# Two attention layers on 128 graphs: value products of two units in one run, output projections spread over the steps

## The reference

```python
# layer 0
nx = _ln(x, ln1_g, ln1_b)
q, k, v = nx @ wq + bq, nx @ wk + bk, nx @ wv + bv        # 8 heads of 32
bias = where(adj > 0, 0.1 * adj * adj, -inf)
attn = softmax(q k^T / sqrt(32) + bias)
x1 = x + ((attn v) @ wo + bo)
x2 = x1 + gelu(_ln(x1, ln2_g, ln2_b) @ w1 + b1) @ w2 + b2   # 256 -> 1024 -> 256
# layer 1, on x2
q, k, v = x2 @ Wq + bq, x2 @ Wk + bk, x2 @ Wv + bv
attn = softmax(where(adj == 0, -inf, q k^T / sqrt(32)))
y = (attn v) @ Wo + bo + x2
out = (y - mean) * rsqrt(var + eps) * gamma + beta
```

## Time and profile before

| what | value |
|---|---|
| runs | 2198.92, 2195.23, 2197.36 us; median 2197.36 |
| profiled execution | 2197.36 us, span 2195.3 us |
| mean granted clock of TensorE | 0.988 of full |
| data moved | 75.74 MB, mean 35 GB/s |
| costliest group | ScalarE's exponentials, 2048 of 393 ns |
| second | GpSimd's products with the inverse, 512 of 1064 ns |

### The profile page before, as it was taken

One profiled execution on the slowest core, in us unless ns is written; L12 is line 12 of the kernel. 1 busy time (PEld: TensorE's weight loads), 2 busy tenths in 40 slices (PEclk: granted clock), 3 DMA queues, 4 the chain that ended last, 5 costly groups with the idle time before them and its releaser, 6 DMA issues.

```text
span 2195.3 us, 58908 instructions
## 1 busy us (share of the span) xinstructions
PE 2150.0 (98%) x20300; PEld 1859.5 (85%) x20300; DVE 1802.1 (82%) x8414; ACT 1683.8 (77%) x5646; POOL 1155.7 (53%) x1266
## 2 busy tenths in 40 slices
PE   8899999999999999999999999999999999999986
PEld 6688888888888888888888888888888888888875
DVE  6688888888888888888888888888888888888774
ACT  5578787778777778877778877788877787877773
POOL 4345655445655455655455555455555455555454
PEclk9999999999999999999999999999999999999997
DMA  4010111011111001111101110101111001110000
GB/s 128 25 35 28 40 33 40 23 31 35 40 33 36 27 28 38 37 36 31 32 28 38 34 39 31 33 26 40 33 40 31 30 28 40 33 40 29 22 14 17
DMA packets 94309, 75.74 MB, mean 35 GB/s; under 512 B 8129, under 2 KB 93761, under 8 KB 94017
## 3 DMA queue, kind: packets, MB, share of 16 engines
q1 hardware_dynamic: 94016, 71.99, 10.7%
HBM read 55.20 MB, written 16.78 MB: 33 GB/s over the span
## 4 chain that ended last, share of the span: by engine, by line
PE 95%; DVE 2%; issue 1%; ACT 1%; POOL 0%; DMA 0%; SPq 0%; POOLq 0%; DVEq 0%
PE p_bank L1124 67%; PE p_heads L1221 10%; PE p_heads L1208 8%; PE p_bank L1240 7%; PE p_bank L1143 4%; ACT scores L650 1%; DVE normed L883 0%; DVE x_two L768 0%; DVE probs_t L920 0%; ACT normed L661 0%; DMA scores<-in_L_gnn_wk 0%; DVE scores L861 0%; DVE adj_c L814 0%; SPq L440 0%; POOL w_up L374 0%
## 5 line engine op out<-in xcount | busy, mean ns | idle before, releaser
L650 ACT ACTIVATE scores<-scores,negmax 128x128 f32<-128x128 f32 x2048 | 793.7, 393 | 25.4 <-DVE negmax L861 25.0
L585 POOL TENSOR_TENSOR scores<-scores,inverse 128x512 f32<-128x512 f32 x512 | 541.9, 1064 | 339.6 <-DVE inverse L872 339.6
L650 ACT ACTIVATION_READ_ACCUMULATOR scores<-scores,negmax 128x1 f32 x2048 | 392.2, 192 | 0.0
L1124 PEld LDWEIGHTS p_bank<-w_down,hidden 128*128 128x128 f32 x3072 | 374.7, 190 | 8.6 <-issue 6.0
L1124 PE MATMUL p_bank<-w_down,hidden 128*128 128x256 f32 x3072 | 381.8, 284 | 0.0
L1124 PE MATMUL p_bank<-normed,w_up 128*128 128x512 f32 x1536 | 370.3, 397 | 1.9 <-DVE normed L883 1.9
L1124 PEld LDWEIGHTS p_bank<-normed,w_up 128*128 128x128 f32 x1536 | 285.0, 189 | 67.6 <-issue 8.4
L1221 PE MATMUL p_heads<-ident,scores 128*128 128x128 f32 x2048 | 313.1, 276 | 8.3 <-DVE negmax L861 3.5
L861 DVE CUSTOM_DVE_ANT_0 scores<-p_heads,adj_a 128x128 f32<-128x128 f32 x1024 | 235.2, 286 | 43.7 <-issue 43.7
L1221 PEld LDWEIGHTS p_heads<-ident,scores 128*128 128x128 f32 x2048 | 241.2, 141 | 35.0 <-DVE negmax L861 11.1
L673 ACT ACTIVATE p_bank<-p_bank,ready_cols 128x512 f32<-128x512 f32 x256 | 169.5, 662 | 131.4 <-PE p_bank L1124 125.9
(11 more groups left out here) (117 smaller groups left out, 3704.5 us busy)
## 6 DMA issues: line engine op xcount, KB each, us to landing
res_a<-in_x SPq DMA_DIRECT2D x32, 512.0 KB, 3.8
out<-res_c SPq DMA_DIRECT2D x128, 128.0 KB, 1.7
x_in<-in_x SPq DMA_DIRECT2D x31, 512.0 KB, 3.8
adj_a<-in_adj SPq DMA_DIRECT2D x32, 256.0 KB, 2.9
adj_c<-in_adj SPq DMA_DIRECT2D x32, 256.0 KB, 2.9
piece_room<-in_L_gnn_w SPq DMA_DIRECT2D x2, 512.0 KB, 8.1
x_two<-in_x SPq DMA_DIRECT2D x1, 512.0 KB, 5.5
res_c<-in_L_gnn_w SPq DMA_DIRECT2D x1, 512.0 KB, 6.3
```

The lines of the kernel that those rows point to most:

```text
L585: nc.gpsimd.tensor_tensor(rows_g, rows_g, inverse[:, step % 2, heads].unsqueeze(2).broadcast_to([P, HC, P]), ALU.mult).then_inc(probs_made, 1)
L650: last = nc.scalar.activation(scores[:, k % 2, h], scores[:, k % 2, h], ACT.Exp, scale=-1.0, bias=negmax[:, k % 2, h:h + 1], accum_out=tot ...
L1124: last = nc.tensor.matmul(dst, stationary(i), moving(j), start=(n == 0), stop=(n == total_n - 1))
```

## The change

V of two units stands in one run, in the odd steps: in step r, V of units r-3 and r-2, and W of unit r-3; W of unit r-2 follows in step r+1. So V and W of the first unit of a pair come one step later than before, V of the second in the same step as before, and its W one step later. Step 1 has both projections of its pair and step 2 has none, so that stage A is complete when the MLP begins. In step 2 the second projection of values (`V A 1`) moves from behind T1 to ahead of T0. Probabilities and heads get a second buffer each (`probs_t`, `heads_t`), and the copies of heads take the 512 columns of both units at once. The normalization for stage M of units 2 and 3 is in step 2 (unit 2 was at the end of step 1). `late` is made from the new places of W as before, so normalization, gain, shift and store of a unit of C come a step later too. SyncE's code is not touched. The core of the diff:

```diff
-    by_step = {}
+    by_step = {k: [] for k in steps}
     for r, k in enumerate(steps):
-        by_step[k] = ([("V", r - 2), ("W", r - 2)] if r >= 2 or pending else []) + (
-            [("T", r - 1)] if r >= 1 or pending else [])
+        by_step[k] += [("T", r - 1)] if r >= 1 or pending else []
+        by_step[k] += [("W", -3)] if r == 0 and pending else []
+        if r % 2 and (r >= 3 or pending):
+            by_step[k] += [("V", (r - 3, r - 2)), ("W", r - 3)]
+            if r == 1:
+                by_step[k] += [("W", r - 2)]
+            elif r < len(steps) - 1:
+                by_step[steps[r + 1]] += [("W", r - 2)]
...
-        early = {1: ("Q", "A", 0), 2: ("V", "A", 0), 4: ("DOWN", 1), 6: ("Q", "C", 0), 7: ("V", "C", 0)}
+        early = {1: [("Q", "A", 0)], 2: [("V", "A", 0), ("V", "A", 1)], 4: [("DOWN", 1)], 6: [("Q", "C", 0)],
+                 7: [("V", "C", 0)]}
...
-        probs_t = sb("probs_t", [P, H, P])
-        heads_t = sb("heads_t", [P, 2, KC, P], F32R)
+        probs_t = sb("probs_t", [P, 2, H, P])
+        heads_t = sb("heads_t", [P, 2, 2, KC, P], F32R)
...
-                nc.scalar.activation(heads_t[:, HI].rearrange("p c n -> p (c n)"), p_bank[bank][:, 0:KC * P],
+                nc.scalar.activation(heads_part(HI, units), p_bank[bank][:, 0:len(units) * KC * P],
...
-                    if k == 2:
-                        for r in s.late.get(k, []):
-                            apply_norm(t, r, GB - 1)
+                    if k == 2 and s.m and s.pending:
+                        apply_norm(t, -1, 2)
+                        apply_norm(t, -1, 3)
...
+            def value_products(t, units):
...
+                for i, r in enumerate(units):
+                    _, _, b = t.unit(r)
+                    for h in range(H):
+
+                        j, c = h % HC, h // HC
+                        last = nc.tensor.matmul(dst[HD * j:HD * (j + 1), (i * KC + c) * P:(i * KC + c + 1) * P],
+                                                values[room(t, stage)][:, b, h * HD:(h + 1) * HD],
+                                                probs_t[:, parity(r), slot_of(c, j), :], start=True, stop=True)
+                last.then_inc(filled[bank], 1)
```

More of the change, by code:

```diff
@@ L88, in __init__ @@
         self.lag, self.tail = lags(self.steps, pending, drain)
-        self.late, waiting = {}, [-3] if pending else []
+        self.pending = pending
+        self.late, waiting = {}, []
         for k in self.steps:
@@ L136, in __init__, with use_units @@
         assert not self.looped or len(self.use) % BANKS == 0
+    def use_units(self, r):
+        return [use[1] for use in self.use if use[0] == "O" and use[1][0] == r]
     def number(self, ops):
@@ L409, in turned_columns, with parity, turned_rows, heads_part @@
             return p_heads[:, 2 * g:2 * g + 2, KC * P:2 * KC * P]
-        def turned_rows(g):
-            return probs_t[:, HC * g:HC * (g + 1)].rearrange("p (a h) n -> p a (h n)", a=2)
+        def parity(r):
+            return (r if r >= 0 else r + STEPS) % 2
+        def turned_rows(r, g):
+            return probs_t[:, parity(r), HC * g:HC * (g + 1)].rearrange("p (a h) n -> p a (h n)", a=2)
+        def heads_part(part, units):
+            first = parity(units[0])
+            return heads_t[:, part, first:first + len(units)].rearrange("p i c n -> p (i c n)")
         def room(t, what):
@@ L1221, in turn @@
                     last = nc.tensor.transpose(turned_columns(g)[:, n // 2, (n % 2) * P:(n % 2 + 1) * P],
-                                               scores[:, par, HC * g + n, :], ident[:, :])
+                                               scores[:, parity(r), HC * g + n, :], ident[:, :])
                 last.then_inc(probs_turned, 1)
-            def lagging(t, op, r):
-                u, stage, b = t.unit(r)
+            def value_products(t, units):
+                bank, dst = take(t, ("O", units))
+                u_last, stage, _ = t.unit(units[-1])
+                pe.wait_ge(turned_out0, u_last + 1)
+                pe.wait_ge(turned_out1, u_last + 1)
+                if t.unit(units[0])[2] == 0:
+                    for i in range(2):
+                        pe.wait_ge(*drained_bank(*made(t, "V", stage, i)))
+                for i, r in enumerate(units):
[6 more added lines that the diff above has]
+                last.then_inc(filled[bank], 1)
@@ new lines, in project @@
+            def project(t, r):
+                for units in t.s.use_units(r):
+                    bank, number = t.bank(("O", units))
+                    pe.wait_ge(drained[bank], number)
+                bank, dst = take(t, ("W", r))
+                w = weight[weights_of[t.unit(r)[1]][3]]
+                three_passes(dst[:, 0:D], [(lambda i, c=c: heads_t[:, i, parity(r), c, :], lambda j, c=c: w[:, j, c, :])
+                                           for c in range(KC)]).then_inc(filled[bank], 1)
@@ L1227, in lagging @@
+            def lagging(t, op, which):
                 if op == "T":
                     for g in range(2):
-                        turn(t, r, g)
+                        turn(t, which, g)
                 if op == "V":
-                    bank, dst = take(t, ("O", r))
-                    pe.wait_ge(turned_out0, u + 1)
-                    pe.wait_ge(turned_out1, u + 1)
-                    if b == 0:
-                        for i in range(2):
-                            pe.wait_ge(*drained_bank(*made(t, "V", stage, i)))
```

49 lines of the change are left out of this document (17 added, 32 removed).

## The result

The changed kernel takes 2447.59 us (median of five runs, 2439.24 to 2448.91), the kernel before 2197.36 us beside it (2193.95 to 2198.92). The ratio is 1.1127, with a 95% interval of 1.1112 to 1.1142: slower by 250 us. The forecast was 2409 us with a range of 2343 to 2455, so the sign and the range hold, and 39 us were missing. The narrower range that it gave for its own mechanism, 2375 to 2445, was missed by 3 us. The profiled execution took 2439.24 us.

What follows compares the result with a forecast made beforehand. TensorE, busy 98% of the span, was taken as the bound. Per turn -0.55 + 4.6 + 2.0 + 0.6 + 0.4 = 7.05 us, times 30 turns 211.5, on 2197.4 gave 2409 us, range 2343 to 2455.

Steps and rivals of the forecast that it cites:

- pairing: TensorE's value products: runs of two units instead of one save 0.55 us per turn with four pairs.
- wait for the load: Step 6: res_a's load behind unit 1's later store delays GpSimd's probabilities; TensorE waits 4.6 us per turn.
- low clock: TensorE after the wait in step 6: the clock drops to 1.2 GHz, costing 2.0 us per turn.
- (a): Step 2 to 3: moved value projection delays ScalarE's row; TensorE waits 0.6 us ahead of the first UP product.
- (b): Step 7 to 0: unit 3's gain, shift and store wait on GpSimd delay probabilities for the transposes, 0.4 us per turn.
- Rival 1: The clock stays at 2.4 GHz through the wait: 5.05 us per turn, 2349 us; chance 0.13.
- Rival 2: Load early enough and other waits hidden, so only the 0.55 us gain per turn counts: 2181 us; chance 0.04.
- Rival 3: Load early enough but (a) and (b) are paid: +0.45 us per turn, 2211 us; chance 0.03.
- Rival 4: Low clock costs 3.5 us per turn, or the load lands a microsecond later: about 2455 us and above; chance 0.07.

Runs made afterwards that it cites:

- experiment 1: Changed kernel with the load of res_a issued ahead of the store of unit 1 on SyncE; 2239.79 us, ratio 1.0189.
- experiment 9: Kernel of experiment 8 with VectorE's transpose copy ahead of step 0's normalization and ScalarE's MLP high parts ahead of the value copy; 2185.52 us, ratio 0.9944.
- experiment 2: Kernel before, without pairing, with only the load of res_a moved behind the store of unit 2; 2383.51 us, ratio 1.0842.
- experiment 3: Changed kernel with 14 unused products of 512 columns added on TensorE ahead of the second half of transposes in step 6; 2385.78 us, ratio 1.0850.
- experiment 6: Kernel of experiment 5 with the second value projection of stage A back behind the second half of transposes in step 2; 2259.76 us, ratio 1.0281.
- experiment 7: Kernel of experiment 5 with the second value projection of stage A between the two halves of transposes in step 2; 2254.22 us, ratio 1.0260.
- experiment 5: Kernel of experiment 1 with GpSimd making step 0's probabilities before the store wait and bias addition of res_c; 2262.27 us, ratio 1.0292.
- experiment 8: Changed kernel with early res_a load, value projection between transpose halves, later res_a bias additions, own semaphore for stores of units 0 and 1; 2203.24 us, ratio 1.0030.

## Why the prediction held, and where its sum was short

Per turn the prediction had 7.05 us; the traces show 74.04 - 66.12 = 7.92. Where the table gives single times, the first three rows are read in the kernels named, and the last three in the trace of experiment 1, in which nothing but the load has moved.

| term | predicted | measured | from |
|---|---|---|---|
| pairing | -0.55 | -0.5 to -0.8 | experiment 9 against before, 65.60 - 66.12, without or with its last wait taken off; the runs alone: four of 1.01 for eight of 0.57 |
| wait for the load | +4.6 | +5.0 | mean W to T1, 5.84 - 0.80 |
| low clock | +2.0 | +2.0 | 74.04 - 67.29 of experiment 1, less 5.84 - 1.08; and directly, 5.6 - 3.59 behind T1 |
| (a) UP of step 3 | +0.6 | +0.6 | V to UP, 1011.45 - 1009.85 = 1.60 instead of 1.01 |
| scores of step 3 | none | +0.25 | 1.04 behind the transposes of inputs, other work 0.79 |
| (b) T1 of step 0 | +0.4 | +0.7 to 0.8 | W to T1, 994.80 - 993.33 = 1.47; mean of the changed kernel 1.60; less 0.80 |

The column adds up to 7.8 to 8.2, about the 7.92 measured; what is left over is in places of 0.1 us and less.

**The load behind the store** was right link by link, and 0.4 too small. The load took longer: 1064.74 - 1060.58 = 4.16 us from issue to user, and 4.1 on the page, where the earlier trace rows had 3.8. GpSimd's wait for it is 143.9 / 30 = 4.8 in the mean, so the turn shown, with 4.59, is one of the shorter ones. Experiments 1 and 2 show this term from both sides: taken out of the changed kernel, and put into the old one.

**The clock** came out as taken, near the middle of its bounds of 0 and 3.5. That it falls and costs something is what the rows behind the waits of 4.89 and 1.71 us gave; that it costs 2.0 and not 1 or 3 was a choice between bounds that no row fixed, and to hit it was in part luck. Rival 1, a clock that stays up, is refuted by the windows, and experiment 3 shows about what it would have given, 2386 us: 62 us less, which is 2.06 per turn. The turns differ, from 1.3 to the 2.7 us of the one shown.

**The waits (a) and (b).** (a) was sized right, but had a companion that the prediction didn't see: with the projection of values gone from behind the transposes of inputs, the scores of step 3 follow these at once and come later by 0.25. In experiment 6, with that projection back, the transposes of inputs take 0.81 again. The likely reason is T1's copy on VectorE: it reads the banks that the scores write, and it ends 0.15 us ahead of the scores here, in step 4 and in experiment 7 alike. No run took that copy away. (b) was 0.3 to 0.4 short, and this is the mis-sized term: the prediction took gain and shift of unit 3 as partly hidden, "as GpSimd is idle for half of the time". The idle time of the earlier trace rows lies elsewhere: from the end of step 7 to T1 of step 0 the engine's row is full, as the rows ahead of experiment 5 show. An average share stood in for a look at that place.

**Rivals 2 and 3** needed a load that is early enough, and the trace has GpSimd's wait for it in all 30 turns. Rival 2 had 16.5 us less than the kernel before for a kernel in which nothing is late. Experiment 9 comes near to that in the loop, with 0.52 x 30 = 16, and has 10.6 over the whole; the first and last turns take the rest. Rival 3 had 2211 us, experiment 1 is 2240: (b) is larger, and 0.3 ahead of T1 in step 6 and 0.25 ahead of the scores of step 3 are to be added, about 0.7 us per turn or 21 us in all when the small gains elsewhere are taken off; the rest lies outside the loop. **Rival 4** (a low clock that costs 3.5 us, or a load a microsecond later, 2455 us) is near in its time, 7 us above the measured one, but not in its cause: the wait was longer by 0.4 us and not by 1, and the clock cost 2.0. The load a microsecond later alone would be 2409 + 30 = 2439 us.

The forecast's own range has a slip: with the wait at 5.2 and the clock at 2.8 its sum is 8.45 us per turn, which is 2451 us and not 2445. The measured time lies below that.

**The 39 us that were missing.** 0.87 us per turn are 26 us. Another 8 are the difference between the profiled execution, 2439.2, and the median. The last 4 or so lie in the first and last turns, which the prediction counted at nothing. This split rests on one trace.

## What to carry to other kernels

When work moves a step later, follow it to the queue that it ends in. A store that waits for it in an in-order row of DMA issues holds back every load behind it, though no line of that row was changed; put loads ahead of stores that wait. Price each wait of several microseconds on a matmul-bound row with the clock that it costs afterwards. And read the idle time of a side engine in the very step to which work is added, not as a share of the span.

## What the hardware showed that was not expected

- The clock fell again after each of the waits of 4.0 to 6.0 us, turn after turn, and what the low level took was not the same each time: 2.7 us in the turn of the changed kernel shown, 0.39 + 0.93 = 1.3 in that of experiment 2 (T1 0.74 instead of 0.35, the next product 2.50 instead of 1.57). These are the ends of a spread that both kernels have, with means of 2.0 and 1.7.
- Shorter waits left the clock alone: experiment 5 has one of 1.6 us ahead of the scores of step 1 in each turn, and its clock is 1.00 from 200 to 2100 us.
- A load of 512 KB right behind a store of 128 KB took 4.1 us to land in the changed kernel and 4.0 in experiment 2, instead of the 3.8 of the kernel before and of experiment 1 (medians of the pages).
- VectorE's normalization of 256 columns took 1.21 to 1.35 us beside GpSimd's bias addition (experiments 8 and 5), and 0.40 where none ran (kernel before). The kernel before had this too, but there the copy behind it was in time. Here is VectorE of the kernel before, in step 0 beside the addition and in step 1 without it:

```profile
1043.86 1.00 DVE L768 TENSOR_SCALAR x_two<-res_a,moments_M,rstd_M 128x256 f32<-128x256 f32 x1
...
1049.65 0.40 DVE L768 TENSOR_SCALAR x_two<-res_a,moments_M,rstd_M 128x256 f32<-128x256 f32 x1
```
